# A macaron of attention and expert blocks on one core: every step of the event list gets its own place

## The chip, the cores and the metric

One core of one Trainium2 chip. The metric is the device time of one execution, in microseconds (us): less is better. The kernel before took 1050.1 us in the median of three runs (1044.61 to 1054.32).

## The reference, cut to what matters

`x` is (4, 512, 128) in float32; everything is float32 in and out.

```python
x = x + 0.5 * _L0_ffn_ref(_layernorm(x), ...)    # 4 batches, no mask, then experts
x = x + _L0_attn_ref(_layernorm(x), ...)         # causal
x = x + 0.5 * _L0_ffn_ref(_layernorm(x), ...)    # as the first, same weights
x = x + 0.5 * _L1_ffn_ref(_layernorm(x), ...)    # dense: relu(h Wi' + h A' B') Wo', for two k
x = x + _L1_attn_ref(_layernorm(x), ...)         # causal
x = x + 0.5 * _L1_ffn_ref(_layernorm(x), ...)
```

Attention has 16 heads of 8 columns over 512 rows: `softmax(q k' / sqrt(8)) v`, with biases. `_L0_ffn_ref` is itself a transformer block:

```python
hn = _layernorm(x, ln1_g, ln1_b);  x = x + attention(hn) @ wo + bo
hn2 = _layernorm(x, ln2_g, ln2_b).reshape(-1, 128)
idx = argmax(hn2 @ gate_w + gate_b)              # 1 of 8 experts for each of 2048 rows
mid = relu(einsum('th,ehf->etf', hn2, w1) + b1)  # 128 -> 512
y = einsum('etf,efh->eth', mid, w2) + b2         # 512 -> 128
return x + y[idx, arange]
```

The second kind of feed-forward, `_L1_ffn_ref`, sends every row through both of two LoRA variants of one 128-512-128 network and weights them with `top_k_values`.

## The kernel before, in words

**Batches and layers.** The six lines of the reference become four attentions of four batches each: batches 0 to 3 (no mask), 4 to 7 (causal), 8 to 11 (no mask), 12 to 15 (causal), a batch being 512 rows. After 0 to 3 come the first experts, after 4 to 7 nothing, after 8 to 11 the experts again and then the dense layer, after 12 to 15 the dense layer. Attentions 4 to 7 and 8 to 11 run as one stretch.

**The event list.** The order of all work is one list, made by `schedule()` before the program is written. An entry is a name, a batch or layer number and a place in it, such as ("p2", 8, (1, 2, 0)). Every engine's program (`pe_program` L555, `act_program` L697, `dve_program` L807, `pool_program` L1122, `sync_program` L1212, which are PE, ACT, DVE, POOL and SP) goes through the same list from front to back and issues its part of each entry, with semaphores between them. So the list fixes in what order each engine meets its work; it fixes no times. An engine that has to wait for something waits with all that stands behind it.

Each job is given a time in *quads* (a quad is four of the 16 heads of one batch), and `segment()` (L146) sorts the jobs by it and puts them between the attention's own events. Quads are counted from the start of the stretch: 16 for the attention of four batches, so 16 is where the tail behind attention 0 to 3 begins, and 32 where the tail behind 4 to 11 does. In the non-masked attentions a quad takes 11 to 12 us.

**Attention.** For a quad, `p1` computes scores with queries on the partitions (PE, L544) whose maxima DVE takes (L896 and L905); `split` and `m` (POOL L1174, PE, ACT, SP) bring the negated maxima into the operands; `p2` computes the scores again with keys on the partitions (PE, L544, exponential on ACT, L738); `pv` multiplies by the values (PE, L620); `evac`, `o`, `onT`, `out` gather, normalise and project. `p1` runs two quads ahead of `p2` (LEAD). In the non-masked attention a p1 or p2 is four matmuls of 128x512.

**Preparation of a batch.** `stats`, `rstd`, `norm` (DVE, POOL, DVE), `hT` (transpose on PE, copy on ACT L711), `q`, `k`, `v` (one matmul of 128x512 each, L575, copied by ACT L720 or DVE), then `qrem`, `krem`, `qmid`, `kmid`, `qlo`, `klo` on POOL, ACT and DVE, which split q and k into bf16 parts (L1114), `keep` on POOL, and twelve `stack` events, DMAs on SP's queue that put the parts into the operands (L1280). PREP has these times for batches inside a stretch, SECOND for its second batch, NEXT for the first two batches of the coming stretch.

**Experts.** The 2048 rows go in two halves for each of the two times, `hm` 0 to 3. Per layer number l: `lstats`, `lrstd`, `xfold`, `lnorm`, `lT`, `gate` make the normed rows and gate values. Per half: `pick`, `rank`, three `place` steps (0 makes the number of each tile's first row's expert, 1 and 2 the row numbers), eight `scatter` events (indirect DMAs by POOL, L1204) that sort the rows, and `xload` (SP). Then 15 tiles of 128 rows: `lay` copies the expert's weights (DVE, L1017), `tt` transposes the rows (PE L664, ACT L765), `up` (PE L669, relu on ACT L772), `dn` (PE L675, DVE L1026), `ysend` (an indirect DMA by POOL, L1209). `yload` (SP) brings the rows back and `yadd` (DVE, L1031) adds them. `load` brings the experts' weights in, at the start.

**Dense.** For l 8 to 15: `lstats`, `lrstd`, `lnorm`, `lT` (PE, and an ACT copy), four units of `fu0` (PE L683, relu on ACT L778) and `fu1` (PE L683, DVE L1038 and L1042), then `fdn` (32 matmuls, L689, sum on DVE L1045). `flip` (L694, two of them) folds the LoRA matrices into the weights. `send` writes the result.

**Around the change.** All times stand in a few constants that serve every batch, half or layer alike: BESIDE and ALONE for the norms, ROUTE_BESIDE and ROUTE_ALONE for the routing, TILE and UNIT for the spacing of tiles and units, and numbers in `schedule()`.

## Time and profile before

| | |
|---|---|
| median of three runs | 1050.1 us (1044.61 to 1054.32) |
| the profiled execution's own time | 1051.72 us |
| its span in the trace | 1049.9 us |
| mean granted clock of PE | 0.956 |
| DVE busy | 779.2 us (74%) |
| ACT busy | 675.5 us (64%) |
| POOL busy | 340.5 us (32%) |
| chain that ended last | PE 51%, DVE 21%, ACT 11%, issue 10% |

The profile is of one execution. "Busy" is the time in which an engine worked on an instruction; PE's share is in the rows below. A granted clock of 1.00 is full speed. The chain is followed back from the last instruction, at each step to what released it. It has no single engine in it, and so the views by stretch and in order of time are the ones to read. In a timeline a line of an instruction gives its start, its length, its engine and line, and in brackets how long the engine had been idle before it and what ended that. "remote" and "issue" are waits that the profile does not tie to another engine's instruction.

The stages, by the time in the trace: attention 0 to 3 up to about 242 us, with the first tiles of experts behind it; experts (hm 0, hm 1) to about 340; attention 4 to 11 to about 690; experts (hm 2, hm 3) to about 792; the dense part to 836; attention 12 to 15 and the last dense part to the end.

### The profile page before, as it was taken

The numbers are of one execution on the slowest core, as the hardware profiler recorded it, in microseconds if no ns is written. First come the engines' busy times: TensorE is split into PE (matmuls) and PEld (weight loads), VectorE is DVE, ScalarE is ACT, GpSimd is POOL, SyncE is SP. The second block draws the span as 40 slices with busy tenths as digits, with TensorE's granted clock in tenths as the row PEclk, the third lists the DMA queues.
The fourth block names the chain that finished last, engine by engine and source line by source line (L and its number), as shares of the span: only waits on it lengthen the run. The fifth ranks groups of instructions, "written<-read, shape, count | busy, mean of one in ns | idle before, by whom it ended". The sixth has DMA issues, their size and how long they took to land.

```text
span 1049.9 us, 25343 instructions
## 1 busy us (share of the span) xinstructions
PE 908.4 (87%) x10020; PEld 481.1 (46%) x10020; DVE 779.2 (74%) x1412; ACT 675.5 (64%) x1470; POOL 340.5 (32%) x603
## 2 busy tenths in 40 slices
PE   2799999899577899998999998886898889999997
PEld 1132333227575455554323332275764545555554
DVE  5889999845356887789899998554665688888555
ACT  2388878686364578777888877874543157667631
POOL 4443322333645222422324113436541032311100
PEclk9599999999899899999999999998898989999999
DMA  4117730010222221112110100102111022110000
GB/s 145 41 42 183 182 98 2 14 48 17 79 81 77 57 56 45 42 44 55 30 43 22 43 2 12 50 14 79 43 41 41 21 62 64 33 34 4 3 22 20
DMA packets 60520, 52.29 MB, mean 50 GB/s; under 512 B 9106, under 2 KB 57362, under 8 KB 60402
## 3 DMA queue, kind: packets, MB, share of 16 engines
q1 hardware_dynamic: 48980, 40.00, 14.2%
q10 hardware_dynamic: 8478, 4.62, 2.1%
q0 software_dynamic: 2944, 6.05, 1.8%
q8 instruction: 79, 1.29, 0.5%
q14 instruction: 39, 0.32, 0.1%
HBM read 13.64 MB, written 11.06 MB: 24 GB/s over the span
## 4 chain that ended last, share of the span: by engine, by line
PE 51%; DVE 21%; ACT 11%; issue 10%; POOL 3%; DMA 2%; another core or an unknown queue 1%; ACTq 0%; DVEq 0%; SPq 0%; POOLq 0%
PE ps L544 14%; PE ps L620 12%; DVE negm L905 8%; ACT pt L738 8%; DVE blockm L896 4%; PE ps L683 3%; PE ps L575 3%; PE ps L669 3%; PE ps L675 3%; PE ps L689 3%; PE ps L550 2%; PE ps L580 1%; PE ps L628 1%; PE ps L638 1%; DVE a_stats L849 1%
## 5 line engine op out<-in xcount | busy, mean ns | idle before, releaser
L738 ACT ACTIVATE pt<-ps 128x512 f32<-128x512 f32 (+1 forms) x896 | 457.5, 566 | 163.6 <-PE ps L544 115.0
L905 DVE TENSOR_REDUCE negm<-ps 128x2 f32<-128x1024 f32 x256 | 300.4, 1218 | 34.4 <-PE ps L544 31.3
L620 PE MATMUL ps<-pt,va 128*32 128x256 f32 (+1 forms) x4352 | 275.3, 342 | 13.4 <-ACT ot L744 5.5
L896 DVE TENSOR_REDUCE blockm<-ps 128x8 f32<-128x1024 f32 (+1 forms) x192 | 195.4, 1042 | 41.5 <-PE ps L544 27.2
L544 PE MATMUL ps<-ks,qs 61*128 61x128 bf16 (+2 forms) x1536 | 174.4, 294 | 37.3 <-DVE negm L905 16.2
L544 PE MATMUL ps<-qs,ks 64*128 64x128 bf16 (+3 forms) x1408 | 169.2, 297 | 9.8 <-ACT parts L720 3.0
L620 PEld LDWEIGHTS ps<-pt,va 128*32 128x32 f32 x4352 | 92.5, 109 | 124.9 <-issue 81.2
L544 PEld LDWEIGHTS ps<-ks,qs 61*128 61x128 bf16 x1536 | 54.8, 95 | 192.7 <-issue 88.7
L1174 POOL CAST mpart<-negm 128x16 bf16<-128x16 f32 x64 | 13.2, 206 | 291.9 <-DVE negm L905 126.1
L772 ACT ACTIVATE stage<-ps,pt 128x128 f32<-128x128 f32 x240 | 68.6, 371 | 48.5 <-PE ps L669 33.7
L544 PEld LDWEIGHTS ps<-qs,ks 64*128 64x128 bf16 x1408 | 58.1, 95 | 65.8 <-ACT pt L738 44.1
L1209 POOL DMA_INDIRECT y_rows<-pt,numbers_y x60 | 70.4, 1173 | 35.2 <-DVE pt L1026 27.1
L669 PE MATMUL ps<-hTm,pt 128*128 128x128 f32 x480 | 68.2, 287 | 15.2 <-DVE pt L1017 10.8
L675 PE MATMUL ps<-pt,stage 128*128 128x128 f32 x480 | 65.3, 280 | 12.6 <-issue 8.4
L669 PEld LDWEIGHTS ps<-hTm,pt 128*128 128x128 f32 x480 | 61.4, 200 | 19.7 <-ACT hTm L765 8.6
L1017 DVE COPY pt<-experts 128x1156 f32 x60 | 46.4, 778 | 30.3 <-PE ps L620 23.4
L675 PEld LDWEIGHTS ps<-pt,stage 128*128 128x128 f32 x480 | 59.6, 195 | 13.9 <-issue 11.4
L683 PE MATMUL ps<-hTa,wk 128*128 128x512 f32 x128 | 62.9, 631 | 3.5 <-DVE stage L1038 2.7
L1114 POOL TENSOR_TENSOR q<-q,parts 128x512 f32<-128x512 f32 x29 | 33.5, 1155 | 86.3 <-ACT parts L720 85.9
L1038 DVE TENSOR_SCALAR stage<-ps,wpk 128x512 f32<-128x512 f32 x32 | 23.8, 745 | 39.5 <-PE ps L683 27.2
L778 ACT ACTIVATE stage<-ps 128x512 f32<-128x512 f32 x32 | 19.0, 597 | 41.1 <-PE ps L683 32.8
L575 PE MATMUL ps<-hT,wpk 128*128 128x512 f32 x64 | 39.5, 709 | 3.2 <-ACT hT L711 2.0
(151 smaller groups left out, 1026.2 us busy)
## 6 DMA issues: line engine op xcount, KB each, us to landing
qs<-parts SPq DMA_DIRECT2D x80, 128.0 KB
ks<-parts SPq DMA_DIRECT2D x77, 128.0 KB
experts<-in_experts SPq DMA_DIRECT2D x8, 578.0 KB, 5.4
...
qs<-mrow SPq DMA_DIRECT2D x128, 6.0 KB
...
```

Source lines behind the costliest of these rows:

```text
L544: ends[s] = pe.matmul(banks[s][:, col:col + c1 - c0], stationary[s][:, i * P:(i + 1) * P], moving[s][:, c0:c1], start=(m_ == 0), stop=(not ...
L575: pe.matmul(b_bank(o), w["w" + name], hT[:, :], start=True, stop=True).then_inc(b_full, 1)
L620: ins = pe.matmul(pv_bank[32 * j:32 * j + 32, q0:q1], va[n % 2][:, kb, value_at(g, j):value_at(g, j) + 32], pt[:, k_, from_:from_ + q1 - q ...
L669: ins = pe.matmul(b_tiles(o)[:, a, :], we[:, number_of(n, at) % NWE, a * P:(a + 1) * P], hTm[:, number_of(n, at) % 2, :], start=True, stop ...
L675: ins = pe.matmul(pair_of(ka)[:, 0, 0:P], mid_e[:, number_of(n, at) % 2, a, :], we[:, number_of(n, at) % NWE, F + a * P:F + (a + 1) * P], ...
L683: pe.matmul(pair_of(ka)[:, 0, :] if kx else b_bank(o), wk[:, kx, at * P:(at + 1) * P], hTa[:, n % 2, :], start=True, stop=True).then_inc(a ...
L738: a.activation(pt[:, k_ % NPT, S * s:S * s + width], b_bank(o + s)[:, 0:width], ACT.Exp).then_inc(b_free, 1)
L772: ins = a.activation(mid_e[:, number_of(n, at) % 2, fb, :], b_tiles(o)[:, fb, :], ACT.Relu, bias=we[:, at_, 2 * F + fb:2 * F + fb + 1])
L896: v.tensor_reduce(blockm[:, g % 2, :, t, PLACES[c_]], pair_of(ka)[:, :, 0:width].rearrange("p s (b c) -> p s b c", c=P), AX, ALU.max, nega ...
L905: v.tensor_reduce(negm[:, g % 2, :, t, c_], pair_of(ka), AX, ALU.max, negate=True).then_inc(a_free, 1)
L1017: v.tensor_copy(we[:, number_of(n, at) % NWE, :], experts[:, bass.ds(next_expert[n], 1), :] .rearrange("p o c -> p (o c)")).then_inc(laid, 1)
L1209: g_.indirect_dma_start(d["y_rows"][n], bass.IndirectOffsetOnAxis(numbers_y[:, r:r + 1], 0), ysb[:, r, :], None).then_inc(y_sent[r], 16)
```

## The change

The constants make room for tables with a place for every step: NORM_AT for the norms of each layer, ROUTE_AT and TILES_AT for each half, Y_AT for loads and sums of y rows, DENSE_AT for each dense layer, NEXT_AT and NEXT for each beginning of a stretch; PREP, SECOND, FLIP_AT, SETUPS and LOADS get other numbers. The set of 2,535 events is the same and so is what each does. What becomes of the order, engine by engine:

- **PE.** hT 1 goes from behind the fifth p1 of batch 0 to behind the second. For most batches k goes four or five jobs later and v five. gate 0 goes earlier. The two flips go from the quad before last of attention 0 to 3 to its last one. In hm 1, up 3 and dn 2 go ahead of hT 4, and q 4 and k 4 a tile later. tt 7 and tt 10 of hm 2 go one place ahead, tt 0 of hm 3 ahead of dn 14 of hm 2, lT 8 and lT 9 of hm 3 seven tiles back. In the dense part unit 9 3, fdn 9 and unit 10 0 go ahead of hT 12, and q 12 and k 12 behind unit 10 1; fdn 10 goes ahead of unit 11 0; v 12 goes behind unit 11 3; hT 13 one job ahead. Units 12 1 to 12 3 stand closer together.
- **DVE.** stats of each batch go two or three jobs ahead. In hm 1 pick goes a job back, and place 0 behind place 1 and place 2; the third weight copy (lay 2) goes ahead of yadd 0, and stats 4 and yadd 1 behind lay 3; norm 5 behind lay 10; yadd 3 two jobs back. place 1 and place 2 of hm 2 go back, lstats 7 and lnorm 7 ahead. In hm 3 place 1 and lay 0 go ahead, yadd 4, yadd 5 and the norms of l 8 and 9 back by several tiles. In the dense part stats 12, norm 12 and stats 13 stand behind the sums of the units that went ahead. lnorm 15 goes ahead of fdn 14.
- **POOL.** keep goes ahead of a split for eight batches. ysend 0 of hm 1 goes ahead of rstd 4, and three more ahead of the splits of q 4 and of rstd 5. ysend 7 and 8 of hm 2 go behind the eight scatters of hm 3. rstd of l 8 and 9 go back, that of l 11 ahead.
- **SP.** Only expert loads change places with other DMAs; the order of the stack DMAs among themselves and to the others stays.
- **ACT.** Copies follow PE's jobs; a few exponentials change places.

```diff
@@ -76,71 +76,112 @@
...
-PREP = [("stats", 7.6), ("rstd", 7.55), ("norm", 7.1), ("hT", 6.9), ("q", 6.7), ("qrem", 6.65), ("k", 6.5),
-        ("krem", 6.45), ("qmid", 6.3), ("kmid", 6.1), ("qlo", 6.05), ("klo", 5.9), ("v", 3.0), ("keep", -3.0)]
+PREP = [('stats', 7.927), ('rstd', 7.55), ('norm', 7.1), ('hT', 6.9), ('q', 6.7), ('qrem', 6.65), ('k', 6.419),
+        ('krem', 6.553), ('qmid', 6.3), ('kmid', 6.1), ('qlo', 6.05), ('klo', 5.851), ('v', 2.951), ('keep',
+        -2.776)]
...
-SECOND = [("hT", 1.4), ("q", 1.3), ("qrem", 1.25), ("k", 1.15), ("krem", 1.1), ("qmid", 1.0), ("kmid", 0.9), ("qlo", 0.85),
-          ("klo", 0.8), ("v", -1.0), ("keep", -7.0)]
-SECOND_STACK, SECOND_EVERY = 1.2, 0.2
-NEXT = [("stats", 0, 0.0), ("rstd", 0, 0.0), ("norm", 0, 0.35), ("hT", 0, 0.5), ("q", 0, 0.65), ("qrem", 0, 0.7),
-        ("k", 0, 0.8), ("krem", 0, 0.85), ("qmid", 0, 0.9), ("kmid", 0, 1.0), ("qlo", 0, 1.0), ("klo", 0, 1.05),
-        ("stats", 1, 1.2), ("rstd", 1, 1.2), ("norm", 1, 1.5), ("v", 0, 2.0)]
-NEXT_STACK, NEXT_EVERY = 0.75, 0.05
...
-SETUPS = [-0.95, -0.6, -0.3, 0.1, 1.1, 2.1]
+SECOND = [('hT', 1.871), ('q', 1.3), ('qrem', 1.25), ('k', 1.15), ('krem', 1.1), ('qmid', 1.0), ('kmid', 0.9),
+        ('qlo', 0.94), ('klo', 0.8), ('v', -1.0), ('keep', -7.0)]
+SECOND_STACK, SECOND_EVERY = 1.056, 0.182
...
+FLIP_AT = 15.132
...
-STACK_FROM, STACK_EVERY = 6.4, 0.25
+STACK_FROM, STACK_EVERY = 6.412, 0.253
...
-LOADS_FROM, LOADS_EVERY = 3.1, 0.5
-BESIDE = [("lstats", 0.35), ("lrstd", 0.35), ("xfold", 0.55), ("lnorm", 0.8), ("lT", 1.3), ("gate", 1.7)]
-ALONE = [("lstats", 0.15), ("lrstd", 0.15), ("xfold", 0.25), ("lnorm", 0.55), ("lT", 0.8), ("gate", 1.05)]
-
-ROUTE_BESIDE = [("pick", 2.0), ("rank", 2.5), ("place", 2.7), ("place", 2.9), ("place", 3.1)], 3.2, 0.15
-ROUTE_ALONE = [("pick", 1.1), ("rank", 1.4), ("place", 1.45), ("place", 1.65), ("place", 1.85)], 1.7, 0.005
-TILE = 0.207
-UNIT = 0.26
-
-
-def tiles_of(hm, at):
-
-    jobs = []
+LOADS_FROM, LOADS_EVERY = 2.931, 0.418
...
+NORM_AT = {0: {'lstats': 5.45, 'lrstd': 5.45, 'xfold': 5.65, 'lnorm': 5.9, 'lT': 6.4, 'gate': 6.581}, 1: {'lstats':
+        9.231, 'lrstd': 9.45, 'xfold': 9.65, 'lnorm': 9.9, 'lT': 10.4, 'gate': 10.8}, 2: {'lstats': 13.45, 'lrstd':
...
+        'lrstd': 37.5, 'lnorm': 37.9, 'lT': 38.15}, 10: {'lstats': 40.2, 'lrstd': 40.2, 'lnorm': 40.6, 'lT': 40.85},
+        11: {'lstats': 41.35, 'lrstd': 41.35, 'lnorm': 41.75, 'lT': 42.0}, 12: {'lstats': 5.662, 'lrstd': 5.615,
+        'lnorm': 6.3, 'lT': 6.8}, 13: {'lstats': 9.85, 'lrstd': 9.85, 'lnorm': 10.3, 'lT': 10.8}, 14: {'lstats':
+        15.25, 'lrstd': 15.25, 'lnorm': 15.7, 'lT': 16.2}, 15: {'lstats': 17.65, 'lrstd': 17.48, 'lnorm': 17.88,
+        'lT': 18.13}}
+ROUTE_AT = {0: {'pick': 11.1, 'rank': 11.6, 'place0': 11.8, 'place1': 12.0, 'place2': 12.2, 'scatter': 12.209,
+        'every': 0.15, 'xload': 15.2}, 1: {'pick': 18.304, 'rank': 18.5, 'place0': 19.259, 'place1': 18.75,
+        'place2': 18.95, 'scatter': 18.8, 'every': 0.005, 'xload': 20.0}, 2: {'pick': 27.1, 'rank': 27.6, 'place0':
+        27.8, 'place1': 28.189, 'place2': 28.389, 'scatter': 28.3, 'every': 0.15, 'xload': 31.2}, 3: {'pick': 34.2,
...
+TILES_AT = {0: {'start': 16.75, 'every': 0.207, 'lay0': 0.35, 'lay': 0.384, 'tt': -0.257, 'dn': 0.22699999999999998,
+        'ysend': 0.277}, 1: {'start': 20.401, 'every': 0.207, 'lay0': 0.35, 'lay': 0.384, 'tt': -0.213, 'dn':
+        0.22699999999999998, 'ysend': 0.216}, 2: {'start': 32.681, 'every': 0.207, 'lay0': 0.35, 'lay': 0.214, 'tt':
+        -0.299, 'dn': 0.22699999999999998, 'ysend': 0.277}, 3: {'start': 36.033, 'every': 0.207, 'lay0': 0.329,
+        'lay': 0.363, 'tt': -0.257, 'dn': 0.22699999999999998, 'ysend': 0.277}}
+Y_AT = {0: {'yload': 20.072, 'yadd0': 20.582, 'yadd1': 20.682}, 1: {'yload': 23.882, 'yadd0': -0.468, 'yadd1':
+        -0.221}, 2: {'yload': 36.197, 'yadd0': 36.597, 'yadd1': 36.697}, 3: {'yload': 39.75, 'yadd0': 40.093,
+        'yadd1': 40.123}}
+DENSE_AT = {8: {'at': 39.75, 'unit': 0.26, 'fdn': 1.05}, 9: {'at': 40.764, 'unit': 0.273, 'fdn': 1.063}, 10: {'at':
+        41.843, 'unit': 0.273, 'fdn': 1.011}, 11: {'at': 44.011, 'unit': 0.221, 'fdn': 1.05}, 12: {'at': 14.2,
+        'unit': 0.121, 'fdn': 1.05, 'send': 1.3}, 13: {'at': 15.391, 'unit': 0.26, 'fdn': 1.05, 'send': 1.3}, 14:
+        {'at': 16.9, 'unit': 0.26, 'fdn': 1.05, 'send': 1.3}, 15: {'at': 18.4, 'unit': 0.26, 'fdn': 1.05, 'send':
+        1.3}}
+NEXT_AT = {4: {'at': 20.651, 'stack': 0.801, 'every': 0.152}, 12: {'at': 41.47, 'stack': 0.801, 'every': 0.136}}
+
+
+def tiles_of(hm):
+
+    T, jobs = TILES_AT[hm], []
     for t in range(SLOTS):
-        up = at + TILE * t
-        jobs += [(up - (0.35 if t < 2 else 2 * TILE - 0.03), "lay", hm, t), (up - TILE - 0.05, "tt", hm, t),
-                 (up, "up", hm, t), (up + TILE + 0.02, "dn", hm, t), (up + TILE + 0.07, "ysend", hm, t)]
+        up = T["start"] + T["every"] * t
+        jobs += [(up - (T["lay0"] if t < 2 else T["lay"]), "lay", hm, t), (up + T["tt"], "tt", hm, t),
+                 (up, "up", hm, t), (up + T["dn"], "dn", hm, t), (up + T["ysend"], "ysend", hm, t)]
     return jobs
 
 
-def routing(hm, at, how):
-    steps, scatter, every = how
-    return [(at + after, name, hm, i - 2 if name == "place" else None) for i, (name, after) in enumerate(steps)] + \
-        [(at + scatter + every * j, "scatter", hm, j) for j in range(TILES)]
...
-def norms(l, at, how):
-
-    return [(at + after, name, l, None) for name, after in how if l < 8 or name not in ("xfold", "gate")]
-
-
-def dense(l, at):
-    jobs = [(at + UNIT * n, name, l, n) for n in range(FB) for name in ("fu0", "fu1")]
-    return jobs + [(at + UNIT * FB + 0.01, "fdn", l, None)]
-
-
-def beginning(n, at):
-
-    return [(at + after, name, n + k, None) for name, k, after in NEXT] + \
-        [(at + NEXT_STACK + NEXT_EVERY * i, "stack", n, which) for i, which in enumerate(STACK)]
+def routing(hm):
+    R = ROUTE_AT[hm]
+    return [(R[name if at is None else f"place{at}"], name, hm, at) for name, at in
+            (("pick", None), ("rank", None), ("place", 0), ("place", 1), ("place", 2), ("xload", None))] + \
+        [(R["scatter"] + R["every"] * j, "scatter", hm, j) for j in range(TILES)]
+
+
+def returns(hm):
+    return [(Y_AT[hm]["yload"], "yload", 2 * hm + b, None) for b in range(2)]
+
+
+def sums(hm):
+    return [(Y_AT[hm][f"yadd{b}"], "yadd", 2 * hm + b, None) for b in range(2)]
+
+
+def norms(l):
+    return [(at, name, l, None) for name, at in NORM_AT[l].items()]
+
+
+def dense(l):
+    D = DENSE_AT[l]
+    jobs = [(D["at"] + D["unit"] * n, name, l, n) for n in range(FB) for name in ("fu0", "fu1")]
+    return jobs + [(D["at"] + D["fdn"], "fdn", l, None)]
+
+
+def beginning(n):
+    at = NEXT_AT[n]["at"]
+    return [(at + after, name, n + k, None) for name, k, after in NEXT[n]] + \
+        [(at + NEXT_AT[n]["stack"] + NEXT_AT[n]["every"] * i, "stack", n, which) for i, which in enumerate(STACK)]
 
 
 def segment(batches, causal_of, jobs):
@@ -212,32 +253,23 @@
     first += [(at, "setup", i, None) for i, at in enumerate(SETUPS)]
     first += [(LOADS_FROM + e * LOADS_EVERY, "load", e, None) for e in range(E)]
     first += [*[(4.0 + hm, "pads", hm, None) for hm in range(4)], (8.0, "late", 0, None), (8.6, "late", 1, None)]
-    first += [(14.2 + 0.3 * f, "flip", f, None) for f in range(FLIPS)]
+    first += [(FLIP_AT + 0.3 * f, "flip", f, None) for f in range(FLIPS)]
     plan = []
-    for m, (batches, end) in enumerate((([0, 1, 2, 3], 16), ([4, 5, 6, 7, 8, 9, 10, 11], 32))):
-        jobs = first if m == 0 else [(-0.6, "yadd", 2, None), (-0.5, "yadd", 3, None)]
+    for m, batches in enumerate(([0, 1, 2, 3], [4, 5, 6, 7, 8, 9, 10, 11])):
+        jobs = first if m == 0 else sums(1)
         for b in range(NB):
-            jobs += norms(4 * m + b, end - 10.9 + 4 * b, BESIDE if b < NB - 1 else ALONE)
-        jobs += routing(2 * m, end - 6.9, ROUTE_BESIDE) + routing(2 * m + 1, end + 1.1, ROUTE_ALONE)
-        jobs += [(end - 0.8, "xload", 2 * m, None), (end + 4.0, "xload", 2 * m + 1, None)]
-        jobs += tiles_of(2 * m, end + 0.75) + tiles_of(2 * m + 1, end + 4.5)
-        jobs += [(end + 4.05, "yload", 4 * m + b, None) for b in range(2)] + \
-            [(end + 7.75, "yload", 4 * m + b, None) for b in (2, 3)]
-        jobs += [(end + 4.45, "yadd", 4 * m, None), (end + 4.55, "yadd", 4 * m + 1, None)]
-        if m == 0:
-            jobs += beginning(4, end + 4.6)
-        else:
-            jobs += [(end + 8.1, "yadd", 6, None), (end + 8.15, "yadd", 7, None)]
-            for b, at in enumerate((4.5, 5.4, 8.1, 9.25)):
-                jobs += norms(8 + b, end + at - 0.05, ALONE)
-                jobs += dense(8 + b, end + 7.75 + 4 * UNIT * b)
-            jobs += beginning(12, end + 9.0)
+            jobs += norms(4 * m + b)
+        for hm in (2 * m, 2 * m + 1):
+            jobs += routing(hm) + tiles_of(hm) + returns(hm)
+        jobs += sums(2 * m) + beginning((4, 12)[m])
+        if m == 1:
+            jobs += sums(3)
+            for b in range(NB):
+                jobs += norms(8 + b) + dense(8 + b)
         plan += segment(batches, causal_of, jobs)
-    end, jobs = 16, []
-    for b, at in enumerate((5.5, 9.5, 14.9, 17.5)):
-        jobs += norms(12 + b, at, BESIDE if b < NB - 1 else ALONE)
-        jobs += dense(12 + b, (14.2, 15.4, 16.9, 18.4)[b])
-        jobs += [((14.2, 15.4, 16.9, 18.4)[b] + 5 * UNIT, "send", b, None)]
+    jobs = []
+    for b in range(NB):
+        jobs += norms(12 + b) + dense(12 + b) + [(DENSE_AT[12 + b]["at"] + DENSE_AT[12 + b]["send"], "send", b, None)]
     return plan + segment([12, 13, 14, 15], causal_of, jobs)
 
```

## Rows read from the trace of the kernel before

**Rows 1.** The page, busy time by engine: us, share of the span, instructions.

```profile
PE 908.4 (87%) x10020; PEld 481.1 (46%) x10020; DVE 779.2 (74%) x1412; ACT 675.5 (64%) x1470; POOL 340.5 (32%) x603
```

**Rows 2.** Busy time by stretch: stretch, length, each engine's busy us, granted clock.

```profile
75.00:200.00 125.00, 114.85 (x1118) 39.60 (x1120) 116.28 (x170) 100.79 (x196) 40.15 (x87) 1.00 0.40 100
...
792.00:836.00 44.00, 35.76 (x161) 23.06 (x162) 24.82 (x59) 10.02 (x18) 6.11 (x8) 0.88 0.14 36
```

**Rows 3.** Timeline of the start: start, us, engine, line, [idle before <-releaser].

```profile
30.50 0.61 PE L544 MATMUL ps<-ks,qs 61*128 61x512 bf16 x2 [0.52 <-DVE negm L905]
...
33.12 2.05 PE L575 MATMUL ps<-hT,wpk 128*128 128x512 f32 x2 [0.42 <-ACT hT L711]
...
35.75 1.23 DVE L905 TENSOR_REDUCE negm<-ps 128x2 f32<-128x1024 f32 x1 [1.78 <-PE ps L544]
```

**Rows 4.** Timeline, the last quads of the first attention.

```profile
218.69 1.12 PE L694 MATMUL ps<-stage 16*128 16x512 f32 x2
...
229.64 9.69 ACT L738 ACTIVATE pt<-ps 128x512 f32<-128x512 f32 x18 [0.79 <-PE ps L544]
```

**Rows 5.** Timeline, first to second expert half.

```profile
279.63 0.36 SPq L1250 DMA_DIRECT2D pt<-sorted  x1
...
282.70 0.69 PE L664 MATMUL ps<-identf,pt 128*128 128x128 f32 x2 [3.69 <-DMA pt<-sorted]
...
292.83 0.69 DVE L1031 SCALAR_TENSOR_TENSOR x<-pt,x 128x512 f32<-128x512 f32 x1 [4.52 <-DMA pt<-y_rows]
...
294.34 1.13 PE L669 MATMUL ps<-hTm,pt 128*128 128x128 f32 x8 [1.92 <-DVE pt L1017]
...
299.68 0.63 PE L569 MATMUL ps<-identf,lnx 128*128 128x128 f32 x4 [3.21 <-DVE lnx L865]
...
317.44 1.13 PE L669 MATMUL ps<-hTm,pt 128*128 128x128 f32 x8 [1.08 <-DVE pt L1017]
```

**Rows 6.** Timeline, indirect DMAs on POOL and DVE's wait beside them.

```profile
265.99 1.46 POOL L1209 DMA_INDIRECT y_rows<-pt,numbers_y  x1 [1.05 <-DVE pt L1026]
...
274.77 0.96 POOL L1204 DMA_INDIRECT sorted<-res,pos  x1 [0.31 <-issue]
...
280.94 0.15 DVE L1025 COPY numbers_y<-stage 128x1 uint32<-128x1 uint32 x1 [6.18 <-remote]
```

**Rows 7.** Timeline, PE at the start of the second attention.

```profile
344.73 0.39 PE L544 MATMUL ps<-ks,qs 61*128 61x128 bf16 x4 [3.06 <-DVE blockm L896]
```

**Rows 8.** Timeline, third to fourth expert half.

```profile
736.94 2.05 PE L669 MATMUL ps<-hTm,pt 128*128 128x128 f32 x8 [0.78 <-ACT hTm L765]
...
743.68 1.13 PE L669 MATMUL ps<-hTm,pt 128*128 128x128 f32 x8 [1.43 <-DVE pt L1017]
...
746.62 1.13 PE L669 MATMUL ps<-hTm,pt 128*128 128x128 f32 x8 [0.81 <-DVE pt L1017]
```

**Rows 9.** Timeline of the dense part.

```profile
797.18 1.09 PE L569 MATMUL ps<-identf,lnx 128*128 128x128 f32 x4 [4.91 <-DVE lnx L865]
...
817.27 0.59 SPq L1280 DMA_DIRECT2D ks<-parts  x1
...
819.61 5.47 PE L689 MATMUL ps<-wo,stage 128*128 128x128 f32 x32 [1.48 <-DVE stage L1038]
...
832.14 3.73 PE L689 MATMUL ps<-wo,stage 128*128 128x128 f32 x32
```

**Rows 10.** Busy time by stretch, in the dense part; columns as in rows 2.

```profile
792.00:797.20 5.20, 0.29 (x2) 0.06 (x1) 4.92 (x16) 0.04 (x1) 2.27 (x4) 0.89 0.00 0
797.20:804.00 6.80, 6.80 (x13) 3.34 (x14) 2.25 (x6) 2.12 (x4) 0.27 (x1) 0.58 0.00 1
```

**Rows 11.** Timeline of the end.

```profile
1028.54 1.04 POOL L1197 TENSOR_TENSOR l_rstd<-l_tmp,minus_half 128x4 f32<-128x4 f32 x1
...
1031.42 1.11 DVE L957 TENSOR_SCALAR hTa<-x,l_mv,l_rstd 128x128 f32<-128x128 f32 x4
...
1032.68 0.63 PE L644 MATMUL ps<-identf,hTa 128*128 128x128 f32 x4 [1.90 <-DVE hTa L957]
```

More of the change, by code:

```diff
@@ new lines @@
+ROUTE_AT = {0: {'pick': 11.1, 'rank': 11.6, 'place0': 11.8, 'place1': 12.0, 'place2': 12.2, 'scatter': 12.209,
+        'every': 0.15, 'xload': 15.2}, 1: {'pick': 18.304, 'rank': 18.5, 'place0': 19.259, 'place1': 18.75,
+        'place2': 18.95, 'scatter': 18.8, 'every': 0.005, 'xload': 20.0}, 2: {'pick': 27.1, 'rank': 27.6, 'place0':
+        27.8, 'place1': 28.189, 'place2': 28.389, 'scatter': 28.3, 'every': 0.15, 'xload': 31.2}, 3: {'pick': 34.2,
+        'rank': 34.5, 'place0': 34.55, 'place1': 34.598, 'place2': 34.9, 'scatter': 34.362, 'every': 0.005, 'xload':
+        36.0}}
```

13 lines of the change are left out of this document (added).

## The prediction, made before the result was known

> **What bounds the kernel now.** I read the page's busy shares first [rows 1]. PE is busy 87% of the span, DVE 74%, so neither has much to give over the whole. Then the busy times by stretch [rows 2]. In the first attention (75 to 200 us) DVE is busy 116.3 of 125 us and PE 114.9. An event that swaps places with its neighbour there finds no idle time to fill. In the dense part (792 to 836) PE works 35.8 of 44 us at a mean clock of 0.88. This and the joints between attention and experts are where the waits are, and the timelines come next, each read for what ended the wait of PE or DVE. The set of events stays the same, 2,535 of them, with every buffer and instruction. So the change can only gain or lose waits, and the sum is made place by place, against the profiled execution's own 1051.7 us.
>
> **Start.** DVE's maxima set the pace; at 35.75 DVE waits 1.78 us, because PE made q of batch 1 late, at 33.12 for 2.05 us, when ACT had copied hT 1 [rows 3]. hT 1 moves from behind the fifth score job to behind the second, and its copy is then done long before PE comes to q. The score jobs come 1.13 apart (30.50 in the row, so 31.6 for the last), and q can start at about 32.1. Gain 1.0 us (0.5 to 1.8), and DVE passes it on.
>
> **Flips.** Two LoRA matmul jobs, 1.12 us each and 0.96 apart from their overlap, leave a stretch in which PE has no pause for one in which ACT runs 18 exponentials in 9.69 us without one [rows 4]. Two times 0.96 is 1.9 us; in the new place PE is nearly full as well, so I take half, 0.9 (0 to 1.9). DVE's step behind each finds DVE idle. The load of the sorted rows (SP) waits for the second flip and starts some 10 us later, at about 235, with the first tile's transpose behind the exponentials, at 240. In the next half the same load took 3.1 us from issue (279.63) to first use (282.70) [rows 5], so it stays hidden.
>
> **First to second expert half (hm 1).** At 292.83 DVE has waited 4.52 us for y rows and only then copies weights for tile 2. PE waits 1.92 us for that copy, and then 3.21 us for the norm of batch 4, with the next tile's matmuls queued behind hT 4 [rows 5]. The change puts the third copy ahead of the y sum: the 1.92 goes. It puts up 3 and dn 2 ahead of hT 4: two times 0.9 us of PE work fall in the 3.21. q 4 and k 4 go behind a tile each. norm 5 goes behind copy 10, which removes a PE wait of 1.08. That makes 4.8. Against it: the norm of batch 4 still follows the y rows, so hT 4 comes no earlier, and the tiles moved forward run out of copies sooner. I take 3.0 (1.0 to 4.8). One price is on the other side. A y send takes 0.96 us in a run without a weight copy and 1.46 beside one [rows 6]; the third copy, now beside the last send, may put the y rows off by its 0.75. That is in the low end. The Trainium skill (SBUF — State Buffer, "Who interferes with whom") says that VectorE in a two-port mode and GpSimd exclude each other for a whole instruction. By it the last send waits for the whole third copy and the term would be 2.3; the two lengths of the sends agree with it.
>
> The place steps of hm 1 come out of order: the one that makes the experts' first tiles goes behind the two that use them, which so read the numbers of hm 0. In time it is 1 us of DVE work moved. The row numbers' step stays behind a dn that PE sets, so the scatters start where they did.
>
> **Second attention, start.** DVE does both y sums in one go, while PE waits 3.06 us for a score maximum [rows 7]. The second sum moves two places back: 0.6 (0 to 0.7).
>
> **Third to fourth half (hm 3).** The same joint: PE waits 1.43 and 0.81 us for the third and fourth copies, behind the y sums, and 0.78 for a transpose that stood behind the last dn of hm 2 [rows 8]. The change moves sums and norm back by several tiles, and copy and transpose forward: 3.0. But it also moves two y sends behind the eight scatters. What such a run does is plain in the trace and has no name there: once some indirect DMAs have gone out without a pause, PE's completions reach DVE late, waits that the trace gives to "remote", 6.18 us for dn 13 of hm 0 [rows 6]. The run in hm 2 grows from 12 DMAs to 14, each 1.26 behind the other (0.96 and a pause of 0.31): 2.5 us more. Net 0.5 (-2.5 to 3.0).
>
> **Dense part.** Here most of it lies. hT 12 waits 4.91 us for a norm that needs fdn 8's sum, while two ready matmul jobs of unit 9 stand behind it [rows 9]. In the 6.8 us after it the granted clock is 0.58 and PE never idle [rows 10]. Further on PE waits 1.48 before fdn 10, which takes 5.47 us, where the same 32 matmuls of fdn 11 take 3.73 [rows 9]. The change sends unit 9's last jobs, fdn 9 and unit 10's first ahead of hT 12, and fdn 10 ahead of unit 11. Walking the new order with the old durations, hT 12 waits about 0.9 instead of 4.9: 4.0. The slow stretch, behind a gap that is gone: 6.8 times 0.42 is 2.9. fdn 10: 1.7 from the clock and 1.5, about the wait ahead of it. Sum 10.1. The ceiling is 12.9: of the 44 us PE worked 35.8, 4.6 of them owed to the slower clock, so 31.1 remain; DVE's 24.8 lie below. The floor is 0, should DVE's units and the norms beside them pace it. The next attention must not come before its operands: their last DMA goes out at 817.27 for 0.59 [rows 9] and was needed at 836. Those 18.7 us shrink by the 10.1 and by some 1.5, since q 12 comes that much later in the new order; 7 remain for the landing, where the sorted rows took 3.1: no bound yet. The skill (TensorE: Matmul & The Clock Gate, "What's actually happening") has it that idleness halves the clock and activity gives it back. By that all 4.6 of the slower clock vanish if the gaps do; the stretch behind the 4.91 agrees, and why fdn 10, behind 1.48 only, was slow is less clear.
>
> **End.** The last norm moves ahead of fdn 14's sum. PE waited 1.90 us for it [rows 11]. It needs the rstd, ready at 1029.6, when DVE's unit is about done too; so its 1.11 is over at 1030.8, where it now ends at 1032.5, and PE, which has waited since 1030.8, goes on. 1.8 (1.0 to 2.6).
>
> **At nothing.** k and v of 14 batches go back by two to five jobs, stats and keep forward, expert loads closer together. Cover: passes run two quads ahead, and both engines are full [rows 2], so a job moved is a job swapped. Without that cover each would cost the job itself, about a flip's 1.12; I allow 2 us both ways for all. Spreading the operand stacking changes nothing: on SP's queue these DMAs stand in the same order, and only loads change places.
>
> **Sum.** 1.0 + 0.9 + 3.0 + 0.6 + 0.5 + 10.1 + 1.8 = 17.9 us. From 1051.7 that leaves 1033.8. The median of the three runs, 1050.1, lies 1.6 lower, so I expect **1032 us**.
>
> **Rivals.** *Given back (chance 0.20).* DVE paces the dense part: the PE gap of 4.9 is closed and mostly opened again behind it, 3 us instead of 10.1; hm 3 loses its 2.5; the rest gives 6. About 6.5 us, 1043 to 1045. For it: in the gap DVE is busy 4.9 of 5.2 us [rows 10], so what moves ahead of the norm makes the norm later. Against: from there to 836 DVE works 19.9 of 38.8.
>
> *The longer DMA run (0.07).* A completion that comes 6.2 us late [rows 6] is now the lot of the last jobs of hm 0 and hm 2. If moving two sends lets the run of 14 reach into hm 3, and the new order in hm 1 puts more jobs beside its run, each one caught costs 6.2. It decides from the third job on: three cost 18.6 and outweigh the 17.9; five make 31 and give 1063, and slower by over 1% takes that many. For it: a wait of 6.2 us for a job of 1.1 has no other match in the rows. Against: only three jobs are left in either half when they begin.
>
> *It does not do what it says (0.03, within the first).* The jobs change places in the list, but each wait that goes is replaced by the same wait one job on, since the y rows and norms come no earlier. It gives 1050.
>
> **Chances.** 0.73 for the forecast, within 1025 to 1039; 0.20 for given back; 0.07 for the DMA run. A measurement here can tell about 1%, 10.5 us, from no change. The upper ends together are 27.7 us, hence 1022, and 1021 with part of the 2 us allowed for k and v. On the other side 1044 takes in half of given back and leaves out the rest and the DMA run. Range 1021 to 1044. Faster 0.73, same 0.20, slower 0.07.
>
> **What would show it.** Right: no PE wait of over 2 us ahead of hT 12, fdn 10 under 4 us, the dense part up to the first scores of batch 12 some 10 us shorter; the third weight copy of hm 1 and hm 3 ahead of the y sum; the last lT right behind fdn 14. Wrong: "remote" waits that grow by more than 2.5 us, a wait for operand DMAs at the first score of batch 12, a new gap on DVE for the out-of-order place step, or longer attention parts, which would mean that k and v did not move for nothing.

## The result, and the profile after

The changed kernel took 1019.67 us in the median of four runs (1019.1 to 1020.92), against 1048.15 for the kernel before: a ratio of 0.9735 (95% interval 0.9707 to 0.9763). That is faster by 28 us, where 18 were forecast, and 1.3 us below the range. (The median before is now one of four runs; it was 1050.1 in three when the forecast was made.) The profiled execution took 1020.19, with a span of 1018.4.

The page after, busy time by engine [rows 1]:

```profile
PE 897.5 (88%) x10020; PEld 477.1 (47%) x10020; DVE 779.7 (77%) x1412; ACT 674.8 (66%) x1470; POOL 342.2 (34%) x603
```

PE works 10.9 us less than before with the same 10,020 matmuls; what it lost is time at the slower clock. The other 20.6 us of the 31.5 by which the two profiled spans differ are waits of PE: it is idle for 120.9 us, before 141.5. Busy time by stretch of the changed kernel, in this order: the first attention [rows 2]; the dense part from ahead of the last units of l 8 to the end of fdn 11; the eight us around hT 12 [rows 10]; one batch's length of the causal attention, from the second quad of batch 5; and the eight us behind the last transpose:

```profile
73.80:198.90 125.10, 114.79 (x1116) 39.33 (x1114) 116.20 (x170) 101.03 (x196) 41.73 (x88) 0.99 0.41 100
770.00:811.80 41.80, 39.07 (x198) 26.06 (x198) 32.75 (x82) 12.37 (x21) 7.38 (x10) 1.00 0.15 39
788.00:796.00 8.00, 7.49 (x24) 3.79 (x24) 5.23 (x9) 5.56 (x10) 1.66 (x2) 1.00 0.12 31
386.86:423.64 36.78, 35.63 (x634) 20.28 (x633) 30.36 (x52) 28.41 (x63) 12.25 (x28) 1.00 0.18 47
1003.00:1011.00 8.00, 7.22 (x20) 3.37 (x20) 4.77 (x7) 2.87 (x5) 0.00 (x0) 1.00 0.11 33
```

The dense part now has PE busy 39.1 of 41.8 us at full clock (198 matmuls in the stretch), where it was 35.8 of 44 at 0.88 (161). The stretch of the first attention is as long as it was. Timelines of the changed kernel: first tiles of hm 1 [rows 5], hT 12 and fdn 10 [rows 9], and the last transpose [rows 11]:

```profile
285.37 2.15 DVE L1049 COPY pt<-experts 128x1156 f32 x3
...
291.37 0.69 DVE L1063 SCALAR_TENSOR_TENSOR x<-pt,x 128x512 f32<-128x512 f32 x1 [3.84 <-DMA pt<-y_rows]
...
293.37 1.13 PE L701 MATMUL ps<-hTm,pt 128*128 128x128 f32 x8 [0.52 <-ACT hTm L797]
...
297.78 0.66 PE L601 MATMUL ps<-identf,lnx 128*128 128x128 f32 x4 [2.38 <-DVE lnx L897]
```

```profile
788.51 0.63 PE L601 MATMUL ps<-identf,lnx 128*128 128x128 f32 x4 [0.99 <-DVE lnx L897]
...
796.28 2.84 PE L721 MATMUL ps<-wo,stage 128*128 128x128 f32 x24
799.30 1.16 PE L721 MATMUL ps<-wo,stage 128*128 128x128 f32 x8 [0.18 <-DVE stage L1074]
```

```profile
1002.84 0.63 PE L676 MATMUL ps<-identf,hTa 128*128 128x128 f32 x4
```

hT 12 waits 0.99 where it waited 4.91, fdn 10 takes its 32 matmuls in 4.0 us plus 0.18 of waiting, and the last transpose has no wait in its row. The third weight copy of hm 1 stands ahead of the y sum (the group of three from 285.37), and hT 4 still waits 2.38 of its 3.21.

By the start of the same event in both traces, each in its own trace's time, the gain grows so: 1.0 us at the third quad of batch 0; 1.8 at the first tiles; 4.7 at the first causal scores; 8.3 when attention 8 begins; 7.2 when attention 11 begins and 9.0 half-way through it; 11.9 at fdn 8; 24.0 at fdn 11; 27.9 at attention 14; 28.0 before the last transpose and 31.5 at the last fdn. Three of these steps are in no term of the forecast: the causal attentions, the middle of attention 11, and 2.8 us inside attention 13.

One thing about the order itself. In hm 1 the steps place 1 and place 2 run ahead of place 0, so by the code they use the first tiles and tile counts that place 0 worked out for hm 0. The events do the same work, but on other numbers. That is right only while no expert needs more tiles of 128 rows in hm 1 than in hm 0. Worked out from the reference's inputs, the counts are 2, 1, 2, 1, 2, 2, 2, 1 and 2, 1, 2, 1, 2, 1, 2, 1 for seed 0, where it holds; for seed 3 expert 6 needs three tiles in hm 1 and has two, and rows would land on the next expert's tiles. Whoever carries the order on should put place 0 first again; what that costs alone was not tried.

### The profile page after: what moved, and what is told of

The parts are those of the page before. It is cut to its first block, busy times and chain, and to the rows that moved or that the text cites. A ratio compares the mean times of both kernels' runs of the same rounds, so it can differ in the third digit from the quotient of the medians.

```text
span 1018.4 us, 25342 instructions
## 1 busy us (share of the span) xinstructions
PE 897.5 (88%) x10020; PEld 477.1 (47%) x10020; DVE 779.7 (77%) x1412; ACT 674.8 (66%) x1470; POOL 342.2 (34%) x603
## 4 chain that ended last, share of the span: by engine, by line
PE 53%; DVE 21%; issue 10%; ACT 10%; another core or an unknown queue 2%; DMA 2%; POOL 1%; DVEq 1%; ACTq 0%; SPq 0%; POOLq 0%
PE ps L576 14%; PE ps L652 13%; DVE negm L937 10%; ACT pt L770 7%; PE ps L715 4%; PE ps L607 3%; PE ps L707 3%; PE ps L701 3%; PE ps L582 3%; DVE blockm L928 2%; PE ps L721 2%; PE ps L660 2%; PE ps L612 1%; PE ps L670 1%
## 5 line engine op out<-in xcount | busy, mean ns | idle before, releaser
L937 DVE TENSOR_REDUCE negm<-ps 128x2 f32<-128x1024 f32 x256 | 300.9, 1219 | 31.0 <-PE ps L576 28.4
L715 PE MATMUL ps<-hTa,wk 128*128 128x512 f32 x128 | 58.6, 599 | 2.3 <-DVE stage L1070 1.6
L797 ACT ACTIVATE hTm<-ps,wpk 128x128 f32<-128x128 f32 x60 | 28.2, 472 | 21.2 <-remote 12.3
```

What stands on the lines that cost most here:

```text
L715: pe.matmul(pair_of(ka)[:, 0, :] if kx else b_bank(o), wk[:, kx, at * P:(at + 1) * P], hTa[:, n % 2, :], start=True, stop=True).then_inc(a ...
L937: v.tensor_reduce(negm[:, g % 2, :, t, c_], pair_of(ka), AX, ALU.max, negate=True).then_inc(a_free, 1)
```

## The experiments

Each kernel is the changed one with one group of places set back, unless said otherwise. "In the trace" means differences of the same event's start against the changed kernel, inside the part that was edited. One execution differs from another by 1 to 4 us, mostly at the joints of the halves, so the trace is read inside a part and the ratios over the whole.

The joints themselves need a measure of their own, and all traces together give one. From the first tile of hm 0 to the first causal scores, the 13 traces with the changed kernel's places there take 85.4 to 89.1 us (mean 86.7, the changed kernel's own 85.8), and the three with the places of before 88.7, 89.5 and 90.6. From the first tile of hm 2 to the first dense unit, the ten traces with the changed kernel's places take 80.2 to 82.0 (mean 81.2, the changed kernel's own 80.2, the lowest), and the three with the places of before 82.0, 82.1 and 82.9. So at a joint one pair of traces can be off by 1 to 3 us.

**PREP back.**

```diff
+PREP = [("stats", 7.6), ..., ("k", 6.5), ("krem", 6.45), ..., ("klo", 5.9), ("v", 3.0), ("keep", -3.0)]
```

> The changed kernel with only PREP set back, so stats, k, krem, klo, v and keep of the ten batches prepared inside a stretch stand where they stood before. Theory A (the cost left out of the forecast: in the causal attentions the places of k and v are not free): 6 to 8 us slower than the changed kernel, about 1026, and the whole of it inside attentions 4 to 7 and 12 to 15, some 0.75 us per batch there. Rival (the forecast's term: a job moved is a job swapped): within 2 us of the changed kernel, 1018 to 1022, and the unforecast gain comes from another group.

1026.79 us (1024.71 to 1027.18), ratio 0.9780 (0.9746 to 0.9814). In the trace 0.68, 0.75, 0.76 and 0.69 us per causal batch from 4 to 7, 0.8 and 0.5 won back in attentions 8 and 9, and 0.8 lost in 12 to 14: 2.5 in all, and 1.7 more at the joint of hm 2 and hm 3, which this edit does not touch. By the ratios it is 4 to 4.7. The term was left out wrongly; its size is nearer to 3 than to the 6 to 8 that I expected.

**Dense part back.**

```diff
+NORM_AT[10] = {'lstats': 40.2, ...}     # and 11
+DENSE_AT[9] = {'at': 40.79, 'unit': 0.26, 'fdn': 1.05}     # and 8, 10, 11
+NEXT_AT[12] = {'at': 41.0, 'stack': 0.75, 'every': 0.05}
```

> The changed kernel with only the dense part between the attentions set back (norms of l 10 and 11, the units of l 8 to 11, the beginning of batch 12). The forecast's term: 10.1 us slower, 1029.8. From the two traces: 12.2 us, 1031.9, the 4.9 us wait ahead of hT 12 back and the slow clock behind it. Rival (given back): only 3 us slower, 1022.7, because the wait would have been made good elsewhere.

1034.0 us (1031.91 to 1034.85), ratio 0.9850 (0.9816 to 0.9885). In the trace fdn 8 to fdn 11 takes 43.4 us, 7.9 more than the changed kernel's 35.5; the kernel before took 47.6 for it. What lies between 43.4 and 47.6 shows for the most part in PE's rows of this kernel, to be read with rows 9:

```profile
788.35 1.09 PE L613 MATMUL ps<-identf,lnx 128*128 128x128 f32 x4 [3.74 <-DVE lnx L909]
...
809.38 3.84 PE L733 MATMUL ps<-wo,stage 128*128 128x128 f32 x32 [1.49 <-DVE stage L1082]
```

The wait ahead of fdn 10 is there (1.49, before 1.48), but this time fdn 10 took 3.84 us and not 5.47, and the slow stretch behind hT 12 lasts 3.4 us instead of 6.8. The kernel with PREP alone, whose dense part is wholly in the order of before, shows the same three numbers (3.74, 3.4, 3.84). So in the order of before, the clock falls behind the wait of 1.48 in one execution and not in another. Put as waits and clock, from fdn 8 to fdn 11: PE is idle 8.2 us before, 7.0 here and 1.2 in the changed kernel, and the slower clock takes 5.1, 1.7 and 0. "Given back" (3 us) is excluded. The ratios give 11 to 12 us for the whole; in this trace the 3.8 that are not in the dense part lie at the joints, which the edit does not touch.

**Norms, routing, tiles and sums of the halves back.**

```diff
+NORM_AT[0] ... NORM_AT[9], ROUTE_AT, TILES_AT, Y_AT for hm 0 to 3, NEXT_AT[4]: the places of before
```

> The changed kernel with norms 0 to 9, routing, tiles and sums of all four expert halves and the beginning of batch 4 set back. The forecast's terms: 3.0 + 0.6 + 0.5, so 4.1 us slower, 1023.8. From the two traces, with the place steps of hm 2 (1.9), the joint of hm 2 and hm 3 (2.8) and hm 1 (4.2): 8 to 9 us slower, 1028. Rival (longer DMA run costs): setting it back gains at the third joint, under 3 us slower in all.

1030.2 us (1029.48 to 1034.23), ratio 0.9821 (0.9780 to 0.9861). In the trace: 4.4 up to the first causal scores, 0.9 in the first y sums behind them, 1.9 in attention 11, 1.8 at hm 3: 9.0 us, where the forecast's terms were 4.1; the ratios give 8 to 9. Of the 4.4, 0.7 come in attention 3, ahead of the first tile, where the forecast had no term, and 3.7 at the joint. Taken against the means above, the joint is worth 2.9 us and hm 3 1.1, so of this trace's numbers some 1.5 us are one execution's difference from another.

**PREP alone on the kernel before.**

```diff
 (everything as before)
+PREP = [('stats', 7.927), ..., ('k', 6.419), ('krem', 6.553), ..., ('klo', 5.851), ('v', 2.951), ('keep', -2.776)]
```

> Everything set back but PREP: the kernel before with only the new PREP. Theory A: 6 to 8 us faster than the kernel before, about 1041.5, since the causal attentions are gained whatever stands around them. Rival: within 2 us of the kernel before.

1046.18 us (ten runs), ratio 0.9967 (0.9948 to 0.9986): 3.5 us (1.5 to 5.5). In the trace against the kernel before, 0.7 to 0.76 per causal batch again, and 1.1 lost in attentions 8 and 9. So the gain is there whatever stands around it, and it is about 3 us.

**Last dense part back.**

```diff
+NORM_AT[15] = {'lstats': 17.65, 'lrstd': 17.65, 'lnorm': 18.05, 'lT': 18.3}     # and 12 to 14, DENSE_AT[12] to [15]
```

> The changed kernel with the last dense part (units of l 12 to 15, norms of 12 to 15) set back. The forecast's term: 1.8 us slower than the changed kernel. Theory B (a removed wait also removes the fall of the clock behind it): 3.5 us slower, of which 1.8 is the wait ahead of lT 15 and 1.7 unit 15's first two jobs and what follows at half clock, and the trace shows a slow stretch near the end that the changed kernel has not. Rival: under 1 us, DVE's sum of fdn 14 being late instead.

1026.46 us (1024.01 to 1027.93), ratio 0.9768 (0.9738 to 0.9797). In the trace 3.7 us: 0.35 in attention 15, 1.80 at the last transpose, 1.52 behind it. Busy time by stretch behind that transpose, in this kernel:

```profile
1009.00:1017.00 8.00, 7.16 (x16) 3.46 (x17) 2.77 (x4) 2.23 (x4) 0.00 (x0) 0.79 0.09 28
```

The granted clock is 0.79 here and 1.00 in the changed kernel's 1003 to 1011, with PE as busy: the wait of 1.90 us and the half-clock stretch behind it come and go together. They do so in the two other traces that have the wait, with 1.7 us behind it in the kernel before and 2.6 in PREP alone. Theory B holds.

**k and v back.**

```diff
-('k', 6.419) ... ('v', 2.951)
+('k', 6.5) ... ('v', 3.0)
```

> The changed kernel with only the places of k and v of the ten batches set back; stats, krem, klo and keep stay in their new ones. Theory A1 (PE's matmuls of k and v stand in the way of the events that feed ACT and DVE): the same 0.7 us per causal batch comes back as when all of PREP went back, 4 to 5 us in all. Rival A2 (it is stats moved out of the crowded quad on DVE): under 1 us, and the loss of 0.7 us per batch stays away.

1022.95 us (1022.4 to 1024.54), ratio 0.9747 (0.9720 to 0.9774). In the trace 0.68, 0.54, 0.54 and 0.48 us for the batches 4 to 7: 2.2 of the 2.9 us that all of PREP back cost there. k and v carry three quarters of it, A1. The 4 to 5 us expected over the whole did not come: by the ratios this kernel is only 0.5 to 1.3 us slower than the changed one. The same moment in the kernel before and in this one, PE at the second job of a quad of a causal batch:

```profile
400.73 0.39 PE L544 MATMUL ps<-qs,ks 64*128 64x384 bf16 x4 [0.29 <-ACT parts L720]
...
402.30 0.64 PE L620 MATMUL ps<-pt,va 128*32 128x256 f32 x8 [0.20 <-ACT pt L738]
```

```profile
393.70 0.39 PE L576 MATMUL ps<-qs,ks 64*128 64x384 bf16 x4 [0.29 <-ACT parts L752]
...
395.26 0.64 PE L652 MATMUL ps<-pt,va 128*32 128x256 f32 x8 [0.20 <-ACT pt L770]
```

PE waits 0.29 for ACT's copy of k, which by the code (L720) reads and so frees a PSUM bank that the scores take next, and 0.20 for the exponential behind it. In the changed kernel both waits are gone from the rows: k comes four jobs later, behind the m job of the quad. PE is nearly full there, 35.6 of 36.8 us, while DVE works 30.4 and ACT 28.4. Still PE waits for a bank held by ACT's two copies of 0.69 and 0.68 us, and where those copies fall was not free.

**place 1 and 2 of hm 2 back.**

```diff
-'place1': 28.189, 'place2': 28.389
+'place1': 28.0, 'place2': 28.2
```

> The changed kernel with place 1 and place 2 of hm 2 back at 28.0 and 28.2, a few us earlier on DVE; nothing else. Theory B: closer together they let PE run dry in the third quad of batch 10, the clock falls for 3.4 us near 640 us and the kernel takes 1.9 us more. Rival (order alone, no clock): about 0.3 to 0.5 us and no slow stretch there. The forecast counted nothing for it.

1024.38 us (1022.9 to 1025.05), ratio 0.9751 (0.9724 to 0.9777). In the trace 1.93 us, all in attention 11, in its first quad (the expectation named batch 10 by mistake). Busy time by stretch, this kernel and then the changed one, of the eight us from the first p2 of batch 11, in which the place steps stand, and the four behind them:

```profile
635.00:643.00 8.00, 5.00 (x49) 1.62 (x51) 7.07 (x14) 5.38 (x11) 4.84 (x8) 0.99 0.09 28
643.00:647.00 4.00, 4.00 (x28) 0.93 (x24) 2.83 (x6) 1.40 (x3) 0.00 (x0) 0.59 0.05 17
```

```profile
633.81:641.81 8.00, 6.70 (x65) 1.98 (x63) 7.33 (x14) 5.88 (x13) 3.54 (x7) 1.00 0.07 20
641.81:645.81 4.00, 2.81 (x29) 1.03 (x30) 3.71 (x6) 2.50 (x5) 1.29 (x2) 1.00 0.10 33
```

With place 1 one score maximum behind place 0 instead of three, PE waits 0.81 and 1.77 us for maxima and works 5.0 of 8 us, then the clock is at 0.59; spread, its longest wait in the eight us is 0.60, it works 6.7 and the clock stays. Four executions with the places of before have such a stretch here (the kernel before, the halves back, PREP alone, this one), the 13 with the new ones have none.

**The new PREP in causal attentions only.**

```diff
-(SECOND if k == 1 else PREP)
+(SECOND if k == 1 else PREP[causal_of[n - 2]])     # PREP[False]: the places of before
```

> An improvement that theory A points to: the new PREP only for batches that are prepared during a causal attention, the places of before for those prepared during a non-masked one (2, 3, 10, 11). Theory A: the 0.8 and 0.5 us that the trace lost in the attentions of batches 8 and 9 come back, 1018.3 in place of 1019.7. Rival (those losses come from v of batch 9 or from elsewhere): no change, 1019.5 to 1020.

1020.94 us (1020.33 to 1022.43), ratio 0.9728 (0.9701 to 0.9754). In the trace the 0.62 and 0.45 us of attentions 8 and 9 come back as expected; 1.5 us lost at the two joints hide them, and the expected 1018.3 did not come.

**Six scatters of hm 3 that are no DMAs.**

```diff
+if n == 3 and at % TB < TB - 1:
+    g_.tensor_tensor(spare[...], minus_half, minus_half, ALU.pow)
+    continue
```

> The changed kernel with six of the eight scatters of hm 3 replaced on POOL by a power of 128x4 elements (1.04 us each in the trace, about as long as a scatter's 0.96); their rows are not sent, so hm 3 works on filler rows, and its y rows are read from those of hm 2. Theory C (a run of indirect DMAs makes PE's completions reach the other engines late): from 706 us on the waits given to remote (6.08 and 5.33 us on DVE) shrink to under 1 us each while the replaced ones stand, and hm 3 begins 2 to 5 us earlier. Rival (POOL being busy, whatever with, or the transfers of the sorted rows): the waits stay as they are.

1013.55 us in one execution, 6.6 below the changed kernel's profile; the joint takes 74.3 us where the changed kernel takes 80.2. Timelines of the joint, changed kernel first, then this one (PE's dn 14, DVE's step behind it, POOL's last send of the run):

```profile
721.98 1.92 PE L707 MATMUL ps<-pt,stage 128*128 128x128 f32 x8
...
724.97 0.96 POOL L1241 DMA_INDIRECT y_rows<-pt,numbers_y  x1 [0.30 <-issue]
...
727.91 0.15 DVE L1057 COPY numbers_y<-stage 128x1 uint32<-128x1 uint32 x1 [5.33 <-remote]
```

```profile
720.23 1.92 PE L708 MATMUL ps<-pt,stage 128*128 128x128 f32 x8
...
722.18 0.15 DVE L1058 COPY numbers_y<-stage 128x1 uint32<-128x1 uint32 x1 [6.02 <-PE ps L708]
...
724.34 0.96 POOL L1245 DMA_INDIRECT y_rows<-pt,numbers_y  x1 [0.30 <-issue]
```

In the changed kernel DVE gets dn 14 six us after its start, in this one two, at the matmul's end, though POOL goes on sending for 3 us. With six DMAs fewer, one scatter and the sends behind it, nothing is late. Of the two waits that were expected to shrink, DVE's for dn 13 went from 6.08 to 1.44; that for dn 14 stays at 6.02, but now because PE itself has waited 4.86 for the sorted rows (5.67 in the changed kernel). The kernel sorts only a quarter of hm 3's rows and reads the y rows of hm 2, so it differs in its data and in SP's load too. This supports theory C, and does not prove it.

**Sends of tiles 7 and 8 ahead again.**

```diff
-'scatter': 34.362
+'scatter': 34.65
```

> The changed kernel with the sends of tiles 7 and 8 of hm 2 ahead of the eight scatters of hm 3 again, as before; only POOL's order changes. The forecast's rival (a run of 14 or 15 costs more than one of 12): this gains, 2.5 us or more at the joint of hm 2 and hm 3. Theory D (the run has the same DMAs either way and its end is what counts; ahead, they only put off the scatters): same end within 0.5 us at the fourth weight copy, or up to 2.5 us slower because the sorted rows come later.

1020.66 us (1016.9 to 1021.49), ratio 0.9735 (0.9709 to 0.9761): as the changed kernel, with an interval of some 2.7 us to either side. The last send of POOL's run in this kernel, and DVE's late step behind it:

```profile
718.75 0.95 POOL L1241 DMA_INDIRECT y_rows<-pt,numbers_y  x1 [0.30 <-issue]
...
721.55 0.15 DVE L1057 COPY numbers_y<-stage 128x1 uint32<-128x1 uint32 x1 [4.49 <-remote]
```

DVE's late step begins 1.85 us after the end of POOL's run here, 1.98 in the changed kernel, 2.05 at both joints before. So the end of the run goes with it. And the run is not the same in any order: with the two sends ahead it holds 12 DMAs (704.31 to 719.70), in the changed kernel 15 (706.31 to 725.93). The joint takes 78.6 us here, and 80.3 in the one other trace with the sends ahead (the two places together, below), against 80.2 to 82.0 with the sends behind. The forecast's rival of the longer run is therefore open: the whole times show no price for it, the joints one of about 1.7 us on the mean, on two traces only.

**hT 1 and flips back.**

```diff
+SECOND = [("hT", 1.4), ...]
+FLIP_AT = 14.2
```

> The changed kernel with hT 1 and the two flips back in their old places. The forecast's terms: 1.0 and 0.9, so 1.9 us slower, 1021.6. From the traces 1.1 at the start and 0.8 at the flips, seen up to the first tile of hm 0. Rival (the first joint gives it back, since the sends and scatters set its end): up to 2 us slower at 240 us and under 1 us at 330 us.

1022.11 us (1019.9 to 1024.74), ratio 0.9739 (0.9710 to 0.9767). In the trace 0.85 at the start, and 0.1 at the flips' places: the quad with the flips is 1.9 us longer wherever they stand (13.0 against 11.1, and 13.3 against 11.5 in the last quad). hT 1 is as forecast; the flips are worth nothing, since PE is as full in the new place.

**Routing earlier, beyond the change.**

```diff
-3: {... 'lnorm': 17.65, 'lT': 17.9, 'gate': 18.15},  1: {'pick': 18.304, ... 'scatter': 18.8}
+3: {... 'lnorm': 17.45, 'lT': 17.6, 'gate': 17.85},  1: {'pick': 17.95, ... 'scatter': 18.45}
```

> An attempt beyond the change: norm and gate of layers 3 and 7 and the routing of hm 1 and hm 3 (pick, rank, place, scatters) 0.1 to 0.35 quads earlier, the rest as changed. Theory D (POOL's run of sends and scatters sets the end of both joints): the scatters begin 2 to 3 us earlier at each and both joints get 1.5 to 3 us shorter, 1014 to 1017. Rival (DVE and PE of hm 0 and hm 2 are full, so what goes ahead puts the tiles back by as much): 1019 to 1021.

1023.45 us (1020.95 to 1024.02), ratio 0.9752 (0.9723 to 0.9781): no gain, and slower than either theory said. In the trace the tiles of hm 0 fall behind by 2.0 us at the sixth and 8.9 at the last, and 3.8 stay at the first causal scores. At hm 3 it is otherwise: the joint takes 78.2 us, 2.1 less than in the changed kernel's trace, and 1.5 of that go to a slow stretch at fdn 8. So the earlier routing may pay in hm 3 alone; that was not tried.

**The changed kernel again, with the two mended places beside it, and v alone back.**

```diff
 (unaltered)  |  PREP by mask and 'scatter': 34.65  |  ('v', 3.0)
```

> The changed kernel itself, unaltered, as the measure for the two beside it on the same chip. 1019.7 us within 1, and the place of each event in the trace within 1 us of the first trace up to the joints of hm 0 and hm 1; what differs more than that is what one execution differs from another.

> The changed kernel with the preparation of before for batches 2, 3, 10 and 11 and the sends of tiles 7 and 8 of hm 2 ahead of the scatters of hm 3. If both traces told of a real gain: 1.6 + 1.6, so about 1016.5. Rival (they are differences between executions at the joints): within 1 us of the changed kernel beside it.

> The changed kernel with only v of ten batches back at 3.0 quads; k stays. If v carries the loss of 0.5 us per batch prepared in a causal attention that the trace showed with k and v back: the same 0.5 at p2 of batches 6, 7 and 8. If k does: under 0.15 there.

The changed kernel again: 1022.21 us (six runs, 1018.31 to 1023.98), ratio 0.9742 (0.9719 to 0.9766). That is 2.5 us over the first median, where at most 1 was expected, and the kernel before measured beside it is 2.3 higher too (1050.47). Both places together: 1020.23 (five runs), ratio 0.9725 (0.9699 to 0.9751): 2 us better, which the intervals do not separate from nothing. v alone back: 1022.66, ratio 0.9740 (0.9714 to 0.9766), and 0.13 us per causal batch in the trace: by subtraction most of the 0.5 is k's; k alone was not set back.

## Why the prediction was wrong, step by step

- **Start**: right. Forecast 1.0, the traces 1.1, undone 0.85.
- **Flips**: forecast 0.9, undone 0.1. Wrong, and without weight: "nearly full as well" was halved where it should have been taken in full. The 0.9 us by which the two profiles differ from attention 3 to the first tile comes back with the halves' places (0.7), not with the flips' (0.1).
- **hm 1 and the start of the second attention**: forecast 3.6. Undone it is 5.3 in one trace, of which 0.7 lie ahead of the tiles, in attention 3, with no term; the joint and the y sums by the means of all traces are 2.9 and 0.7, so 3.6. That is as forecast. The steps are the ones named: PE's wait of 1.92 for the third weight copy is gone (the next tile's is 0.52, for another engine), and PE waits 2.38 instead of 3.21 at hT 4. The wait of 1.08 for copy 10 did not go as forecast: it is 0.81 for copy 9. The price feared for the third copy did not come: the last send took 1.22 us beside the copies in both kernels, and the y rows were there 4.4 us after its end in both. The out-of-order place step cost no time to be seen.
- **hm 3**: forecast 0.5, undone 1.8 in one trace and 1.1 by the means. The experiments don't separate the forecast's two parts. The run did grow, from 13 DMAs to 15 (12 with the sends ahead), and its price of 2.5 us is neither shown nor excluded: the whole times say nothing, the joints say about 1.7.
- **Place steps of hm 2**: no term. They gain 1.9 in the trace (0.9 to 1.7 by the ratios). The forecast went by rows 2, where DVE is full and an exchange of neighbours finds nothing to fill; but extra steps close together on a full DVE leave PE without work, and then the clock falls.
- **Dense part**: forecast 10.1. Undone it is 7.9 in one trace and 11 to 12 by the ratios (0.9850 against 0.9735 and 0.9742). The mechanism is the one told: of the 7.9, 5.8 are waits of PE (forecast 4.0 + 1.5) and 1.7 are the clock (forecast 2.9 + 1.7). The size of the clock share depends on the execution: it was 5.1 in the profile of before and 1.7 in both traces of the same order taken later.
- **k and v at nothing**: this step failed. "Passes run two quads ahead, and both engines are full [rows 2], so a job moved is a job swapped" was argued from a stretch of the non-masked attention and used for the causal one too. There the places in PREP are worth 0.7 to 0.75 us per batch, of which k and v carry three quarters; in all it is 2.5 in the trace of PREP undone, 3.5 alone on the kernel before, and 4 to 4.7 by the ratios of PREP undone, against an allowance of 2. I read no row of the causal attention: there DVE is idle for a fifth of the time, and PE waits for a bank that ACT holds.
- **End**: forecast 1.8 (1.0 to 2.6), undone 3.7. The wait is 1.80 as forecast; the 1.5 behind it is the half clock that follows such a wait, which I had counted in the dense part and forgot here. This step failed too.

The terms undone add up to 0.9 + 5.3 + 1.9 + 1.8 + 7.9 + 2.5 + 3.7 = 24.0 us, against the forecast's 17.9; with the means in place of one trace at the two joints it is 22.3. What the forecast lacked, beside k and v, is therefore the clock at the end and in attention 11, not the joints. The medians are 28.5 apart, and 28.3 on the second occasion (1050.47 and 1022.21); the two profiled executions are 31.5 apart, since that of before lay 3.6 above its median. The last 4 to 6 us are not pinned to a place. They fit what the runs of before show: they scatter from 1044.6 to 1054.5, and its profile has slow stretches (behind hT 12 twice as long, at fdn 10, and one in batch 13) which other executions of the same order lack. The one in batch 13 also stands in two of the experiments and in no other. Over the 35 executions of the kernel before that were measured beside the experiments, time and mean granted clock (0.951 to 0.962) go together, with a correlation of -0.73. That these falls of the clock are where the rest lies is likely, and not shown by an experiment. The Trainium skill (TensorE: Matmul & The Clock Gate, "What's actually happening") says that the throttled state is the default and activity releases it; both pairs here agree, 0.79 against 1.00 at the end and 0.59 against 1.00 in attention 11.
